# Reordering two projections, two evictions and the routing work inside the steps of a fused adaLN, attention and mixture-of-experts kernel

## The chip, the core and the metric

The kernel runs on one core of a Trainium2 chip. The metric is the device time of one execution in microseconds (us), the median of three runs. The core has five engines that run their own instruction streams in program order and meet at semaphores: TensorE (PE; its weight loads are listed as PEld), VectorE (DVE), ScalarE (ACT), GpSimd (POOL) and SyncE (SP), which here only issues DMAs.

## The reference, cut to what matters

```python
x: (8, 512, 128)                                  # 8 batches, 512 tokens
mod = silu(c) @ wmod                              # sa, ca, ga, sb, cb, gb per batch
h = layernorm(x) * (1 + ca) + sa
q, k, v = einsum('bsx,xAnh->Abnsh', h, w)         # 16 heads of 64
a = (q + q_bias) @ k.T * h**-0.5
a = a + relative_causal((q + q_bias) @ emb.T)     # sinusoid positions, 32 frequencies
o = softmax(where(mask, a, -1e9)) @ v
x = x + ga * (o @ out_kernel + out_bias)
h = layernorm(x) * (1 + cb) + sb
score = softmax(h @ Wg + bg)                      # 16 experts, top 1, capacity 256
x = x + gb * expert(h)[slot] * gate               # dropped where over capacity
```

The relative term is folded into the key product: each query row carries 64 further features (made from the "positional product" g), each key row 64 sines and cosines.

## The kernel before, in words

The attention is 64 **steps** j = 8b + a: batch b from 0 to 7, pair of heads a from 0 to 7. "Step a" below means that pair in any batch. A step has eight **tiles** k = 0 to 7: head k // 4 of the pair, query block 3, 2, 1, 0 (512, 384, 256, 128 keys wide). The stages of different steps overlap, each engine going through its own `step` function:

- TensorE (`step`, L933): for each tile the scores (`scores`, L823: three fp32r products of high and low parts, L835, and for query block 0 one plain fp32 product, L832), the transposes of step j-1's probabilities (L845), and once per step `project_v` (L820), `project_out` of step j-2 (L872), `project_q` of step j+1 (L797, ahead of tile 3), `project_k` of step j+1 (L797, behind tile 6) and `weighted`, probabilities times values of step j-1 (L865, behind tile 7). In even steps `project_g` (L797, operands named gwhi, gwlo) makes the positional product for two later steps, between tile 7 and `weighted`. Small products of the second half of the layer stand in single places: `turn_x` (step 2, tile 3), `turn_a` (1, 5), `turn_h` (3, 5), `logits` (4, 4; L893), `places` (5, 4).
- VectorE (`step`, L1367): for each tile the mask and row maximum (`scores`, srow and nmax, L1167), then `evac_q` (qx, L1191, tiles 3 and 4), `recip` of the first head (L1179, tile 4), pieces of the other work by (a, k): `residual` (1, 3), `residual2` (1, 7), `xhat1` (1, 5 and 6), `gating` (4, 5; L1257 to L1261), `low` (vlo, 4, 6), `place` (5, 5; L1280 to L1285), `route` and `index` (6, 1 and 2). Behind the tiles: `low_k(j+1, 0)` (klo, L1206), `evac_g` (g, L1200), `recip` of the second head, `evac_g`.
- ScalarE (`step`, L643): for each tile the exponential (`exps`, L612), evictions of transposes (`evac_pt`, L621), `normed` (hn, L565, step 2 behind tile 4), `second` (h2T, L631, step 3 behind tile 6); `evac_k(j+1, 0)` (khi and kx, L578 and L579) behind tile 6 and `evac_k(j+1, 1)` behind tile 7, then `evac_o`.
- GpSimd (`turn`, L458): splits queries into high and low parts (`split_q`, L445 and L447), divides the probabilities (`divide`, L454), and for the experts `modulate`, `gated` and the indirect stores of rows (`scatter`, L437), two tiles of 128 rows in step 6 and two in step 7, on its own DMA queue.
- SyncE: `spread` (L295) sends g to the query tiles for each step; stores and weight loads between.

What joins them around the change. PSUM bank `prb[0]` holds first the query product, then the key product: `project_k` waits until both `evac_q` have read it (`qe`). Bank `prb[1]`, also called `xtb`, holds in turn the value product, the small products and the positional product: `project_g` waits for `normed` (`hn`) in step 2, for the first instruction of `gating` (`lge`) in step 4, for `evac_v` (`ve`) otherwise. Score tile k needs tile k-2 to have been read by VectorE (`tt`), there being two score banks. Tile 0 of a step waits for the first half of the low queries (`ql`, at least 2j+1) and of the low keys (`kl`, at least 2j+1), which `low_k(j, 0)` of the step before sets; `low_k` needs `evac_k` (`ke`), and this needs `project_k` (`kp`).

Ahead of the steps TensorE runs loops of 128x128 bf16 products with no use but to keep it busy (`idle`, L758 to L761): 36, then 30, then 16 of them (L788), the last loop ahead of the first query product. Behind the steps a tail finishes the last batch and then runs the 16 experts.

Of the kernel before, what the change touches and what calls it, by code (L numbers as in the profile page):

```python
# [41 lines left out]
NJ = B * PAIRS  # L42
# [32 lines left out]
def program(nc, x_d, wall_d, wv_d, cols_d, wo_d, bo_d, wg_d, bg_d, w1_d, w2_d, b2_d, wmod_d,  # L75
            consts_d, ktab_d, gtab_d, out_d):
    ctx = ExitStack()
    with ctx:
# [115 lines left out]
        s = {n: sem("s_" + n) for n in names}  # L194
# [174 lines left out]
        def _(gp):  # L369
# [88 lines left out]
            def turn(b, first, last):  # L458
                for a in range(PAIRS):
                    j = 8 * b + a  # L460
                    if first and a in (1, 2):
                        first_pair(a - 1)
                        copy(0, a - 1)
                    if first and a == 3:
                        low_wk(4, PAIRS, 2)
                    if not last:
                        if a == 1:
                            root(0, b + 2)
                        if a in (5, 6):
                            copy(b + 1, a - 5)  # L470
                    if not first:
                        if a == 4:
                            modulate(b)
                        if a == 5:
                            gated(b)
                        if a == 6:
                            scatter(b, (0, 1))
                        if a == 7:
                            scatter(b, (2, 3))
                    after = not (last and a == PAIRS - 1)  # L480
                    if after:
                        split_q(j + 1, 0)
                    divide(j, a % 2, 0)
                    if not first and a == 2:
                        root(1, b)
                    if after:
                        split_q(j + 1, 1)

                    divide(j, a % 2, 1, *([("scat", 64 * b)] if a == 7 and not first else []))

# [27 lines left out]
        def _(act):  # L518
# [124 lines left out]
            def step(j, par, b, a, first, last):  # L643
                before, after = not (first and a == 0), not (last and a == PAIRS - 1)
                for k in range(8):
                    if before and 1 <= k < 6:
                        evac_pt(j - 1, k)
                    exps(j, par, k)
                    if not before:
# [11 lines left out]
                    if k == 6 and a == 3 and not first:  # L661
                        second(b)
                    if after and k == 6:
                        evac_k(j + 1, 0)
                    if k == 6 and a == 4 and not first:
                        gates(b)
                if after:
                    evac_k(j + 1, 1)
                if before:
# [59 lines left out]
        def _(pe):  # L729
# [48 lines left out]
            def turn_x(n, out=xtb):  # L778

                pe.wait_ge(s["xn"], n + 1)  # L780
                for q in range(QT):
# [5 lines left out]
                      start=True, stop=True).then_inc(s["mod_mm"], 1)  # L787
            idle(16)  # L788

# [143 lines left out]
            def step(j, par, b, a, first, last):  # L933
# [4 lines left out]
                for k in range(8):  # L938
# [28 lines left out]
                    if (a, k) == (2, 3) and not last:  # L967
                        pe.wait_ge(s["ve"], j + 4)
                        turn_x(b + 1)
                    if (a, k) in ((1, 5), (3, 5), (4, 4), (5, 4)) and not first:  # L970
                        pe.wait_ge(s["ve"], 8 * B if last and a >= 5 else j + 4)
                        if last and a >= 5:
                            pe.wait_ge(s["gq"], NJ)
                        (turn_a, None, turn_h, logits, places)[a - 1](b)
                    if k == 6 and after:
                        if first and a in (0, 3):
                            pe.wait_ge(s["kwh"], 1 if a == 0 else 2)
                            pe.wait_ge(s["kwl"], 1 if a == 0 else 2)
                        pe.wait_ge(s["qe"], 2 * j + 4)
                        project_k(j + 1, n, m)  # L980
                    if not before:
                        first_step(k)
                    if k == 7 and a % 2 == 0 and j + 2 < NJ:
                        if a == 2 and not last:
                            pe.wait_ge(s["hn"], b + 2)
                        elif a == 4 and not first:
                            pe.wait_ge(s["lge"], b)
                        else:
                            pe.wait_ge(s["ve"], j + 4)
                        project_g(j // 2 + 1)  # L990
# [87 lines left out]
        def _(dve):  # L1078
# [198 lines left out]
            def place(b):  # L1277
# [3 lines left out]
                                       base[:, None, :].to_broadcast([P, QT, E]), ALU.add))  # L1281
                dve.tensor_tensor(base[:, :], base[:, :], xtb[:, QT * E:(QT + 1) * E], ALU.add).then_inc(s["prx"], 1)
                dve.wait_ge(s["prx"], b)
                link(dve.tensor_tensor(lgt[:, 0, :], lgt[:, 0, :], oh16[:, :], ALU.mult))
                link(dve.tensor_reduce(where, te(lgt[:, 0, :]), AX.X, ALU.add))  # L1285

            def route(b):

                link(dve.tensor_scalar(late, where, float(CAP), float(NOWHERE), ALU.is_ge, ALU.mult))
# [41 lines left out]
            def after_attention(b, a, k):  # L1331
# [9 lines left out]
                if (a, k) in ((3, 1), (3, 2)):  # L1341
                    xhat2(b, range(2 * k - 2, 2 * k))
                if (a, k) == (4, 5):
                    gating(b)
# [15 lines left out]
            def step(j, par, b, a, first, last):  # L1360
                before, after = not (first and a == 0), not (last and a == PAIRS - 1)
                for k in range(8):
# [23 lines left out]
                    if not last:  # L1386
                        before_attention(b + 1, a, k)
                if after:
                    low_k(j + 1, 0)
                places = a % 2 == 0 and j + 2 < NJ  # L1390
                if places:
                    evac_g(j // 2 + 1, 0)
                recip(j, par, 1)
                if places:
                    evac_g(j // 2 + 1, 1)

            def low_wo():
# [151 lines left out]
```

## Time and profile before

| | us |
|---|---|
| median of 3 runs | 932.68 |
| lowest, highest | 932.37, 938.14 |
| profiled execution, its own time | 937.85 |
| span of the profiled execution | 935.7 |
| TensorE busy | 884.9 (95% of the span) |
| VectorE, ScalarE, GpSimd busy | 701.6, 664.4, 584.4 |
| mean granted clock of TensorE | 0.983 |

The span runs from the first to the last instruction on the core; the execution's own time is 2.15 us more. The granted clock is a share of full speed (2.4 GHz). All times in the trace count from the start of the span. A step is read from its first score product (L835 behind the last L865) to the next one. The steps take up the span from about 25 to 833 us; the tail and the experts the rest.

### The profile page before, as it was taken

Reading aid. Unit: us, or ns where it says so; the run is one execution under the profiler, and the core shown is the slowest. Engines: PE = TensorE matmul, PEld = TensorE weight load, DVE = VectorE, ACT = ScalarE, POOL = GpSimd, SP = SyncE. Lnnn points to the kernel's source line nnn. Section 1 sums busy time; section 2 is a strip of 40 time slices with the busy share of each in tenths; the row PEclk is TensorE's granted clock in tenths of the full one; section 3 lists DMA queues with packets and bytes.
Section 4 is the critical chain, followed back from the end, with each engine's and each line's share of the span. In section 5 each row is a group of like instructions: output and inputs, shape, how many; then the busy total and the mean of one; then the engine's idle time right before and its main releaser. Section 6 shows DMA issues by size and latency. Waiting matters only on the chain. (4 is left out here: it accounts for less than half of the span.)

```text
span 935.7 us, 18012 instructions
## 1 busy us (share of the span) xinstructions
PE 884.9 (95%) x5515; PEld 676.6 (72%) x5515; DVE 701.6 (75%) x2115; ACT 664.4 (71%) x1843; POOL 584.4 (62%) x917
## 2 busy tenths in 40 slices
PE   7799999999999999999999999999999999998994
PEld 6666777777777777777777767777677777666994
DVE  3678778787887778787878787877877777853784
ACT  3587777877778777877787778777787777750551
POOL 3365655777557766667577765776676757553354
PEclk7799999999999999999999999999999999999998
DMA  7223332112010111011100111010101110005671
GB/s 285 57 80 91 91 86 57 46 46 69 18 37 24 49 32 38 19 40 41 43 23 23 48 33 28 19 42 23 43 18 29 34 43 23 24 16 194 221 219 42
DMA packets 36513, 56.01 MB, mean 60 GB/s; under 512 B 7447, under 2 KB 21512, under 8 KB 36161
## 3 DMA queue, kind: packets, MB, share of 16 engines
q1 hardware_dynamic: 32624, 46.16, 17.5%
q0 software_dynamic: 3072, 5.94, 1.8%
q10 hardware_dynamic: 720, 2.75, 0.9%
q8 instruction: 45, 0.74, 0.3%
q14 instruction: 52, 0.42, 0.1%
HBM read 23.96 MB, written 16.82 MB: 44 GB/s over the span
## 5 line engine op out<-in xcount | busy, mean ns | idle before, releaser
L612 ACT ACTIVATE prob<-srow,nmax 128x512 f32<-128x512 f32 (+3 forms) x512 | 286.2, 559 | 150.6 <-DVE nmax L1167 147.7
L1167 DVE CUSTOM_DVE_ANT_0 srow<-bank,consts 128x512 f32<-128x512 f32 (+3 forms) x512 | 247.0, 488 | 111.1 <-issue 98.3
L454 POOL TENSOR_SCALAR prob<-prob,rsum 128x128 f32<-128x128 f32 (+3 forms) x512 | 263.3, 532 | 46.7 <-DVE rsum L1179 45.1
L845 PE MATMUL bank<-consts,prob 128*128 128x128 f32 x1280 | 201.8, 272 | 0.4 <-POOL prob L454 0.2
L621 ACT ACTIVATE pt<-bank 128x384 f32<-128x384 f32 x318 | 159.5, 502 | 22.2 <-PE bank L845 18.0
L845 PEld LDWEIGHTS bank<-consts,prob 128*128 128x128 f32 x1280 | 158.4, 141 | 23.0 <-POOL prob L454 1.1
L835 PE MATMUL bank<-khi,qhi 128*128 128x512 f32 (+2 forms) x384 | 158.2, 412 | 15.9 <-POOL qlo L447 13.2
L445 POOL CAST qhi<-qx 128x384 fp32r<-128x384 f32 x128 | 68.3, 534 | 167.4 <-PE bank L835 115.9
L865 PE MATMUL bank<-pt,v 128*64 128x512 f32 (+3 forms) x1024 | 152.0, 439 | 0.1
L447 POOL TENSOR_TENSOR qlo<-qx,qhi 128x384 fp32r<-128x384 f32 x128 | 128.9, 1007 | 10.8
L1206 DVE SCALAR_TENSOR_TENSOR klo<-bank,khi 64x512 fp32r<-64x512 f32 x128 | 88.0, 687 | 58.1 <-ACT kx L579 56.1
L835 PE MATMUL bank<-khi,qlo 128*128 128x512 f32 (+2 forms) x384 | 130.4, 339 | 0.0
L835 PE MATMUL bank<-klo,qhi 128*128 128x512 f32 (+2 forms) x384 | 130.1, 339 | 0.0
L865 PEld LDWEIGHTS bank<-pt,v 128*64 128x64 f32 x1024 | 68.0, 136 | 84.0 <-issue 70.3
L612 ACT ACTIVATION_READ_ACCUMULATOR prob<-srow,nmax 128x1 f32 x512 | 96.9, 189 | 0.0
L835 PEld LDWEIGHTS bank<-khi,qhi 128*128 128x128 f32 x384 | 73.0, 190 | 32.9 <-POOL qlo L447 18.6
L1191 DVE TENSOR_SCALAR qx<-bank,pbias 64x512 f32<-64x512 f32 x126 | 94.0, 746 | 2.1
L578 ACT ACTIVATE khi<-bank 64x512 fp32r<-64x512 f32 x128 | 74.8, 584 | 7.6 <-PE bank L797 6.0
L835 PEld LDWEIGHTS bank<-khi,qlo 128*128 128x128 f32 x384 | 72.7, 189 | 5.6
L835 PEld LDWEIGHTS bank<-klo,qhi 128*128 128x128 f32 x384 | 73.8, 192 | 2.8
L797 PE MATMUL bank<-hhi,whi 128*128 128x512 f32 x118 | 57.3, 486 | 6.7 <-DVE qx L1191 2.8
L832 PEld LDWEIGHTS bank<-kx,qx 128*128 128x128 f32 x256 | 44.0, 189 | 21.5 <-DVE nmax L1167 15.2
(193 smaller groups left out, 1475.5 us busy)
## 6 DMA issues: line engine op xcount, KB each, us to landing
qx<-g SPq DMA_DIRECT2D x252, 64.0 KB, 2.0
xbuf<-fill SPq DMA_DIRECT2D x16, 385.0 KB, 4.3
x<-xbuf SPq DMA_DIRECT2D x16, 385.0 KB, 3.6
raw<-in_w SPq DMA_DIRECT2D x16, 256.0 KB, 3.0
prob<-in_w SPq DMA_DIRECT2D x16, 256.0 KB, 4.3
out<-row SPq DMA_DIRECT2D x8, 256.0 KB, 2.6
x<-in_x SPq DMA_DIRECT2D x1, 1792.0 KB, 14.9
modb<-mod_rows SPq DMA_DIRECT2D x8, 192.0 KB, 3.7
```

What stands on the lines that cost most here:

```text
L445: gp.tensor_copy(qhi[:, h, :], qraw(j, h)[:, P:S]).then_inc(s["qh"], 1)
L447: gp.tensor_tensor(qlo[:, h, :], qraw(j, h)[:, P:S], qhi[:, h, :], ALU.subtract).then_inc(s["ql"], 1)
L454: end = gp.tensor_scalar(part, part, rsum[:, par, 4 * h + q:4 * h + q + 1], 1.0, ALU.mult, ALU.mult)
L578: act.activation(khi[0:HD, h, :], prb[0][h * HD:(h + 1) * HD, :], ACT.Copy, scale=C_QKV)
L612: act.activation(prob[:, par, h, QOFF[q]:QOFF[q] + P * (q + 1)], srow[:, k % 4, 0:P * (q + 1)], ACT.Exp, bias=nmax[:, par, k:k + 1], scale ...
L621: act.activation(pt[:, h, KOFF[g]:KOFF[g] + GW[g]], source[:, 0:GW[g]], ACT.Copy)\
L835: last = pe.matmul(out, a[:, h, (q - 1) * P:q * P], b[:, h, 0:P * (q + 1)], start=(i == 0), stop=(i == 2))
L845: last = pe.transpose(out[:, n * P:(n + 1) * P], prob[:, par, h, QOFF[q] + k * P:QOFF[q] + (k + 1) * P], ident)
L865: last = pe.matmul(otb[h * HD:(h + 1) * HD, k * P:S], v[:, g, k, at + h * HD:at + (h + 1) * HD], pt[:, h, KOFF[k]:KOFF[k] + S - k * P], st ...
L1167: dve.tensor_tensor_reduce(out=srow[:, k % 4, 0:w], in0=scb[k % 2][:, 0:w], in1=mask[:, S - w:S], scale=-1.0, scalar=BIG, op0=ALU.add, op1 ...
L1191: dve.tensor_scalar(qraw(j, h)[0:HD, :], prb[0][own, :], pbias[own, a:a + 1], CQ, ALU.add, ALU.mult)\
L1206: dve.scalar_tensor_tensor(klo[0:HD, h, :], prb[0][h * HD:(h + 1) * HD, :], C_QKV, khi[0:HD, h, :], ALU.mult, ALU.subtract).then_inc(s["kl ...
```

## The change

TensorE: in even steps `project_g` moves from behind tile 7 to behind tile 6, and `project_k` from behind tile 6 to behind tile 7, directly ahead of `weighted`; odd steps stay. `logits` moves from tile 4 to tile 3 of step 4. In the very first step `project_g` waits for the first value eviction in place of the fourth. The last warm-up loop has 40 products in place of 16.

ScalarE: in odd steps `evac_k(j+1, 0)` goes ahead of the exponential of tile 6; in even steps both `evac_k` stand behind tile 7.

VectorE: `gating` moves from tile 5 to tile 4 of step 4; the wait and the last two instructions of `place` (step 5) move to the front of `route` (step 6); in even steps `low_k(j+1, 0)` goes behind both `evac_g` and `recip`.

GpSimd: the four indirect stores of a batch, two each in steps 6 and 7, become one each in steps 6 and 7 and in steps 0 and 1 of the next batch, save for the last group taken inside the steps; the wait for them moves with them.

```diff
@@ GpSimd, turn
-                        if a == 6:
-                            scatter(b, (0, 1))
-                        if a == 7:
-                            scatter(b, (2, 3))
+                        if a >= 6:
+                            scatter(b, (2 * a - 12, 2 * a - 11) if last else (a - 6,))
+                    if b > 1 and a < 2:
+                        scatter(b - 1, (a + 2,))
...
-                    divide(j, a % 2, 1, *([("scat", 64 * b)] if a == 7 and not first else []))
+                    divide(j, a % 2, 1, *([("scat", 64 * b - 64)] if a == 1 and b > 1 else []))
@@ ScalarE, step
+                    if after and k == 6 and a % 2:
+                        evac_k(j + 1, 0)
                     exps(j, par, k)
...
-                    if after and k == 6:
-                        evac_k(j + 1, 0)
                     if k == 6 and a == 4 and not first:
                         gates(b)
                 if after:
-                    evac_k(j + 1, 1)
+                    for h in range(a % 2, 2):
+                        evac_k(j + 1, h)
@@ TensorE, before the steps
-            idle(16)
+            idle(40)
@@ TensorE, step
-                    if (a, k) in ((1, 5), (3, 5), (4, 4), (5, 4)) and not first:
+                    if (a, k) in ((1, 5), (3, 5), (4, 3), (5, 4)) and not first:
...
-                    if k == 6 and after:
+                    if k == 7 - a % 2 and after:
...
-                    if k == 7 and a % 2 == 0 and j + 2 < NJ:
+                    if k == 6 and a % 2 == 0 and j + 2 < NJ:
                         if a == 2 and not last:
                             pe.wait_ge(s["hn"], b + 2)
                         elif a == 4 and not first:
                             pe.wait_ge(s["lge"], b)
                         else:
-                            pe.wait_ge(s["ve"], j + 4)
+                            pe.wait_ge(s["ve"], j + 4 if before else 1)
                         project_g(j // 2 + 1)
@@ VectorE, place and route
+
+            def route(b):
+
                 dve.wait_ge(s["prx"], b)
                 link(dve.tensor_tensor(lgt[:, 0, :], lgt[:, 0, :], oh16[:, :], ALU.mult))
                 link(dve.tensor_reduce(where, te(lgt[:, 0, :]), AX.X, ALU.add))
-
-            def route(b):
-
@@ VectorE, after_attention
-                if (a, k) == (4, 5):
+                if (a, k) == (4, 4):
                     gating(b)
@@ VectorE, step
-                if after:
+                places = a % 2 == 0 and j + 2 < NJ
+                if after and a % 2:
                     low_k(j + 1, 0)
-                places = a % 2 == 0 and j + 2 < NJ
                 if places:
                     evac_g(j // 2 + 1, 0)
                 recip(j, par, 1)
                 if places:
                     evac_g(j // 2 + 1, 1)
+                if after and a % 2 == 0:
+                    low_k(j + 1, 0)
```

## Rows read from the trace of the kernel before

**Rows 1.** windows over the eight steps (pairs of heads 0 to 7) of batch 3; columns: stretch, length, busy us per engine, clock

```profile
332.67:345.39 12.72, 12.55 (x76) 9.10 (x74) 9.92 (x34) 9.76 (x29) 7.42 (x13) 1.00 0.05 12
345.39:358.48 13.09, 12.14 (x77) 9.12 (x75) 11.42 (x31) 9.45 (x27) 8.37 (x14) 1.00 0.15 36
358.48:371.47 12.99, 12.83 (x78) 9.50 (x78) 9.78 (x34) 10.20 (x29) 7.32 (x13) 1.00 0.19 42
371.47:383.81 12.34, 11.83 (x77) 9.06 (x75) 9.63 (x29) 9.93 (x27) 8.13 (x14) 1.00 0.15 37
383.81:396.63 12.82, 12.82 (x82) 9.96 (x82) 10.12 (x28) 10.38 (x31) 9.98 (x14) 1.00 0.03 7
396.63:409.06 12.43, 11.84 (x81) 8.97 (x79) 10.59 (x36) 9.44 (x27) 8.65 (x14) 1.00 0.16 39
409.06:421.49 12.43, 12.29 (x74) 9.04 (x74) 9.53 (x31) 9.94 (x29) 8.28 (x14) 1.00 0.11 37
421.49:433.25 11.76, 11.62 (x73) 8.66 (x71) 8.56 (x25) 9.23 (x27) 10.13 (x16) 1.00 0.23 67
```

**Rows 2.** timeline of the end of step 3; columns: start, us, engine, line, what

```profile
380.92 2.37 PE L865 MATMUL bank<-pt,v 128*64 128x512 f32 x16
...
381.10 0.49 ACT L612 ACTIVATE prob<-srow,nmax 128x256 f32<-128x256 f32 x1
...
382.25 0.57 ACT L578 ACTIVATE khi<-bank 64x512 fp32r<-64x512 f32 x1
...
383.02 0.68 DVE L1206 SCALAR_TENSOR_TENSOR klo<-bank,khi 64x512 fp32r<-64x512 f32 x1 [1.60 <-ACT kx L579]
...
383.77 0.19 PEld L835 LDWEIGHTS bank<-khi,qhi 128*128 128x128 f32 x1 [0.72 <-POOL qlo L447]
```

**Rows 3.** timeline of VectorE in step 5

```profile
405.99 0.25 DVE L1284 TENSOR_TENSOR lgt<-lgt,oh 128x64 f32<-128x64 f32 x1
...
406.52 0.42 DVE L1167 CUSTOM_DVE_ANT_0 srow<-bank,consts 128x256 f32<-128x256 f32 x1
...
408.26 0.68 DVE L1206 SCALAR_TENSOR_TENSOR klo<-bank,khi 64x512 fp32r<-64x512 f32 x1 [1.10 <-ACT kx L579]
```

**Rows 4.** timeline of the second half of step 2

```profile
367.14 0.76 ACT L565 ACTIVATE hn<-bank,modT 128x512 f32<-128x512 f32 x1
...
367.23 0.19 PEld L797 LDWEIGHTS bank<-hhi,whi 128*128 128x128 f32 x1 [0.37 <-DVE qx L1191]
...
368.28 0.48 PE L797 MATMUL bank<-hhi,gwhi 128*128 128x512 f32 x1
```

**Rows 5.** timeline of the second half of step 4

```profile
390.47 0.69 DVE L1167 CUSTOM_DVE_ANT_0 srow<-bank,consts 128x512 f32<-128x512 f32 x1 [0.17 <-issue]
390.50 0.96 PE L893 MATMUL bank<-wg,h2T 128*128 128x16 f32 x8
...
392.22 0.56 DVE L1167 CUSTOM_DVE_ANT_0 srow<-bank,consts 128x384 f32<-128x384 f32 x1
...
392.71 0.22 DVE L1257 TENSOR_TENSOR lgt<-bank,bg 128x64 f32<-128x64 f32 x1
...
393.30 0.38 PE L832 MATMUL bank<-kx,qx 128*128 128x128 f32 x2
...
393.72 0.41 DVE L1167 CUSTOM_DVE_ANT_0 srow<-bank,consts 128x256 f32<-128x256 f32 x1
...
394.32 2.38 PE L865 MATMUL bank<-pt,v 128*64 128x512 f32 x16
...
396.06 0.73 DVE L1200 SCALAR_TENSOR_TENSOR g<-bank,gbias,gtab 128x512 f32<-128x512 f32 x1
```

**Rows 6.** windows at the start of the program, with the granted clock (PEclk)

```profile
12.57:15.98 3.41, 1.36 (x17) 0.90 (x16) 1.01 (x1) 3.35 (x7) 2.42 (x2) 1.00 0.89 336
15.98:33.05 17.07, 14.65 (x74) 12.08 (x75) 8.42 (x16) 4.99 (x16) 4.30 (x6) 0.50 0.25 103
```

**Rows 7.** timeline of TensorE, the last warm-up loop

```profile
12.86 1.07 PE L761 MATMUL bank<-ones 128*128 128x128 bf16 x16
```

## The prediction

> **What bounds the kernel now.** I read first the share of the span by engine: TensorE is busy 95%, no other engine over 75%. Then I cut one batch into its eight steps [rows 1]. They repeat from batch to batch within 0.05 us, so one batch stands for seven. The reader is to see that TensorE is full in steps 2, 4 and 6, and short by 0.95, 0.51 and 0.59 us in steps 1, 3 and 5; step 7 has no such hole and takes 11.76 us. So gains can only come from the holes, and every wait that is put into steps 2 and 4 is paid in full.
>
> What makes the holes? In step 3 the timeline shows TensorE coming to the next step's first scores at 383.77, with a wait that the view puts down to the low queries [rows 2]. By the code the first tile needs only their first half, which was made 4 us before. The instruction that ends 0.07 us ahead is klo, the low keys: 383.02 + 0.68 = 383.70. They wait for khi and kx, which ScalarE takes up at 382.25, behind two other activations, though the key product was long done. `weighted` started at 380.92 and takes 2.30 (394.32 to the next step at 396.62, [rows 5]), so TensorE was free at 383.22. The hole is 0.58. In step 5 it is 12.43 - 11.76 = 0.67 [rows 1], again behind klo [rows 3]. In step 1 VectorE is busy 11.42 of 13.09 us [rows 1], and without a pause in the second half, so ScalarE's order can't help there.
>
> **The change part by part.**
>
> *Odd steps, high keys first.* In step 3 khi can start where the exponential now starts, at 381.10 in place of 382.25 [rows 2]: klo ends 1.15 us sooner, more than the hole of 0.58, and TensorE's 2.30 of `weighted` set the end. Same in step 5, hole 0.67. The two delayed exponentials end about 0.6 us into the next step; the first row maximum is due about 1.1 us into a step and ScalarE has some 1 us of idle time ahead of its first exponential, which covers them. Gain 7 x 0.58 + 7 x 0.67 = 8.8 us. Batch 0's odd steps give about 0.5 (0 at the least, two holes like these at the most). Step 7 has no hole: nothing. Step 1: nothing, VectorE's other work covers it.
>
> *Step 2, the positional product behind tile 6.* It writes the bank that `normed` reads, and hn ends at 367.14 + 0.76 = 367.90 [rows 4]. Nothing of the change makes hn earlier. The key product now starts at 367.23; in its place TensorE holds until 367.94, and what follows it (tile 7, the other product, `weighted`) is the same work in another order. Of the 0.71, 0.05 to 0.1 was spent waiting at tile 7 anyway. Cost 0.62, in batches 0 to 6 (the last has no `normed`): +4.3.
>
> *Step 4, logits and gating one tile earlier.* `logits` takes TensorE from 390.50 to 391.32 [rows 5], and now stands ahead of tile 4: its row maximum on VectorE moves from 390.47 to 391.29. From there VectorE goes through evac_q and `recip` to tile 5, 392.22 - 390.47 = 1.75 later, so to 393.04; but `gating` now stands ahead of tile 5, and takes 392.71 to 393.72, 1.01. Tile 5's maximum starts at 394.05 and is done at 394.61. Tile 7 reuses that score bank and waits for it: 394.66 in place of 393.30 [rows 5]. From tile 7 to the step's end stand a product and `weighted`, 1.02 to 1.08 and 2.30: the step ends at 398.04, not 396.62. Cost 1.42. The second chain is as long: VectorE in the new order has tile 6, vlo, tile 7, g, `recip`, g, klo behind 394.05, some 3.9 us by their pitches in the same step, and ends at 398.0. Seven batches: +9.9. Batch 0 has no gating, but in its step 4 VectorE's other pieces already end the step with klo, and klo goes behind two g and a `recip` (0.66 + 0.1 + 0.65, estimated from the row of g): +1.4. The bound from below for both steps is 0, should the held time be covered by something that I don't see; from above 0.4 more per step 4, if both chains add. I take the middle since both chains give the same number.
>
> *Other even steps.* In steps 0 and 6 tile 7 waits for tile 5's maximum before and after; a product stands between and one behind, whichever it is. Nothing in step 0. Low keys last: g is now read before the key product is even done, so klo follows about 12.4 us into a step of 12.72 [rows 1], hidden behind `weighted` with about 0.2 to spare (that cover gone, each 0.1 costs 0.1 in 14 steps). In step 6 the two instructions taken from `place` cost 406.52 - 405.99 = 0.53 [rows 3] in a stretch with about 0.35 of idle time: +0.18 in six batches, 1.1. In the last batch's step 6 there is no positional product to trade with, and the key product moves from beside a wait to the path: 0.9. In step 5 that same 0.53 is in front of klo no more, but the floor of 11.76 is TensorE's.
>
> *GpSimd.* It is busy 7.42 and 8.37 us in steps 0 and 1 [rows 1] and idle in the middle of each, waiting for queries; one indirect store of about 1 us fits. The wait for the stores moves to step 1's second `divide`, by when they have landed. What is behind it, the transposes of step 2, has 2 us to spare. The stores also stand behind nothing on SyncE's queue. g is ready earlier, but SyncE's copies of it wait for the same scores: nothing.
>
> *Warm-up.* Sixteen products took 1.07 us [rows 7] at the full 2.4 GHz; 24 more take some 1.3, inside the pause before the first query product. From 12.57 to 15.98 the clock was full while TensorE worked only 1.36 of 3.41 us, and then it was at its half level, 1.2 GHz, for 17.07 us, 14.65 of them busy [rows 6]. At full clock those would take half: 7.3 us is the most to be had, -0.35 (the loop at half clock reaching past the pause) the least. I take 5.2, which is also how far the profiled execution, 937.85, lies above the median of 932.68; I read that difference as this stretch, and so credit the median itself with nothing more. The Trainium skill, page "TensorE: Matmul & The Clock Gate", section "What's actually happening", says that warming up costs time and not a number of products, that its point moves from run to run, and advises not to fit to a count; by it the loop brings nothing dependable, and an execution like the profiled one would end at 946.2.
>
> Sum: -8.8 - 0.5 + 4.3 + 9.9 + 1.4 + 1.1 + 0.9 = +8.3. Against the profiled execution: 937.85 + 8.3 - 5.2 = 941.0; against the median: 932.68 + 8.3 + 0 = 941.0.
>
> **The rivals.** (1) *The waits in steps 2 and 4 are covered, and it gets faster.* It decides on whether hn and `gating` come before TensorE has finished tile 6 (366.8 in step 2). For it: VectorE and ScalarE are idle 25% of each step. Against it: both chains start from TensorE's own tile 4 and have nothing idle inside. Then 4.3 and 9.9 fall away: 941.0 - 14.2 = 926.8, and 925.4 without batch 0's. (2) *Low keys end every even step late.* If the estimate of their slack is short by 0.3 to 0.4: 14 to 20 steps, +5: 946. For it: the order puts them behind four instructions; against: the sum leaves 0.2. (3) *The half clock stays in the median*: 941.0 + 5.2 = 946.2. (4) *The start gives more than 5.2*: up to 3 more, 938. (5) *Odd steps don't gain*, since the delayed exponentials hold up ScalarE: +8.8, 950; against it the idle time ahead of each first exponential.
>
> **How the numbers follow.** A change of 1% is what a measurement of this kernel can tell from none: 923.4 and 942.0. The forecast has 0.60 (936 to 946; 0.37 of it below 942.0, 0.23 above), rival 1 has 0.13 (0.04 below 923.4), rival 2 0.08, rival 3 0.07, rival 4 0.08, rival 5 0.04. Faster 0.04; same 0.37 + 0.09 + 0.08 = 0.54; slower 0.23 + 0.08 + 0.07 + 0.04 = 0.42. The range is 932 to 947: it leaves out most of rival 1, and rival 5.
>
> **What would show it.** In the new trace steps 3 and 5 take 11.8 us, with no wait at their end; step 2 takes 13.6, TensorE idle ahead of the positional product until hn; step 4 takes 14.2 to 14.4, with two holes, one ahead of the positional product (behind `gating`'s first instruction) and one ahead of tile 7; steps 0, 1, 6 and 7 take 12.7, 13.1, 12.6 and 11.8. The granted clock at the start is full for longer. Wrong would be a step 4 under 13.3, or a step 3 over 12.2: then VectorE's order or ScalarE's doesn't set what I say it does.

## The result, and the profile after

The changed kernel takes 940.77 us in the median of 8 runs (938.08 to 942.94); the kernel before, beside it, 933.67. The ratio is 1.0067 [1.0046, 1.0089]: slower by 7.1 us, and within 1%. The prediction was 941.0.

The profiled execution of the changed kernel took 942.51 us, with a span of 940.6 and a mean clock of 0.986; before it was 937.85, 935.7 and 0.983. The page's line of shares shows how little an average tells here:

```profile
PE 885.7 (94%) x5539; PEld 675.8 (72%) x5539; DVE 700.1 (74%) x2115; ACT 664.0 (71%) x1843; POOL 587.4 (62%) x917
```

All engines but GpSimd are within 1.5 us of their sums of before, and so the time is in the waits. The windows over the eight steps of batch 2 (same columns as [rows 1]) show where:

```profile
231.61:244.31 12.70, 12.43 (x75) 9.03 (x73) 10.47 (x34) 9.79 (x29) 8.84 (x15) 1.00 0.10 28
244.31:257.42 13.11, 12.12 (x76) 9.12 (x75) 10.95 (x30) 9.70 (x27) 9.19 (x15) 1.00 0.19 52
257.42:271.02 13.60, 12.71 (x77) 9.59 (x77) 10.38 (x34) 10.18 (x29) 7.84 (x14) 1.00 0.14 38
271.03:282.79 11.76, 11.76 (x76) 9.04 (x75) 8.91 (x27) 9.37 (x26) 7.27 (x13) 1.00 0.15 36
282.79:296.81 14.02, 13.37 (x83) 9.95 (x81) 10.69 (x31) 10.96 (x33) 10.92 (x17) 1.00 0.05 12
296.82:308.59 11.77, 11.77 (x80) 8.94 (x79) 9.31 (x31) 9.31 (x26) 7.79 (x13) 1.00 0.14 33
308.59:321.23 12.64, 12.39 (x75) 9.03 (x73) 10.50 (x33) 9.72 (x29) 8.53 (x15) 1.00 0.09 27
321.23:332.99 11.76, 11.63 (x72) 8.65 (x70) 8.15 (x24) 9.23 (x26) 8.33 (x14) 1.00 0.19 52
```

Steps 3 and 5 have lost their holes (TensorE 11.76 of 11.76, before 12.34 and 12.43). Step 2 grew from 12.99 to 13.60, step 4 from 12.82 to 14.02. Over all batches, from the first score of one step to that of the next:

| step | 0 | 1 | 2 | 3 | 4 | 5 | 6 | 7 | sum |
|---|---|---|---|---|---|---|---|---|---|
| predicted | 0 | 0 | +4.3 | -4.3 | +11.3 | -4.9 | +2.0 | 0 | +8.3 |
| measured | -0.11 | +0.09 | +4.69 | -5.29 | +9.52 | -4.94 | +2.19 | -0.36 | +5.8 |

(The sums run from batch 0's step 2 on and are in us; each number is rounded; batch 0's -0.5 is halved over steps 3 and 5.) The stretch ahead of batch 0's step 2 took 54.29 us for 56.02, and what follows the steps 0.8 more.

Three cells of the measured row hold something that is not the change. In single steps VectorE takes up one row maximum 0.36 us later than in the same step of the other batches, and the step is longer by as much: step 4 of batch 4 and step 7 of batch 6 in the kernel before (13.19 and 12.12 us), step 2 of batch 3 in the changed one (13.96). Every kernel here with the stores and `place` as before has these two, every one with them as changed has that one; no row says what the cause is. Without it step 2 is at +4.3, step 4 at +9.9, step 7 at 0 and the sum at +6.2.

**End of step 3**, the timeline of batch 3 after:

```profile
382.25 2.38 PE L866 MATMUL bank<-pt,v 128*64 128x512 f32 x16
...
382.43 0.57 ACT L578 ACTIVATE khi<-bank 64x512 fp32r<-64x512 f32 x1
...
383.06 0.50 ACT L612 ACTIVATE prob<-srow,nmax 128x256 f32<-128x256 f32 x1
...
383.20 0.68 DVE L1207 SCALAR_TENSOR_TENSOR klo<-bank,khi 64x512 fp32r<-64x512 f32 x1 [0.44 <-ACT kx L579]
...
384.56 0.50 PE L836 MATMUL bank<-khi,qhi 128*128 128x512 f32 x1
```

klo used to end 0.07 us ahead of the next scores [rows 2]. Now it ends at 383.88, 0.68 ahead, and the scores come 2.31 behind the start of `weighted`: TensorE's own work sets the end.

**Second half of step 2**, batch 2:

```profile
266.10 0.76 ACT L565 ACTIVATE hn<-bank,modT 128x512 f32<-128x512 f32 x1
...
266.91 0.19 PEld L798 LDWEIGHTS bank<-hhi,gwhi 128*128 128x128 f32 x1 [1.10 <-ACT hn L565]
...
267.82 0.19 PEld L798 LDWEIGHTS bank<-hhi,whi 128*128 128x128 f32 x1
```

The step's first score starts at 257.42. hn ends at 266.86, 9.44 us into it, where it ended before (367.90 - 358.48 = 9.42, [rows 4, 1]), but the product with gwhi is now the one that is next in line, and it waits until 266.91.

**Second half of step 4**, batch 3 again; its first score starts at 384.56:

```profile
390.25 0.96 PE L894 MATMUL bank<-wg,h2T 128*128 128x16 f32 x8
...
392.14 0.69 DVE L1168 CUSTOM_DVE_ANT_0 srow<-bank,consts 128x512 f32<-128x512 f32 x1 [1.07 <-issue]
...
393.87 0.23 DVE L1258 TENSOR_TENSOR lgt<-bank,bg 128x64 f32<-128x64 f32 x1
394.01 2.60 POOL L454 TENSOR_SCALAR prob<-prob,rsum 128x128 f32<-128x128 f32 x4 [1.22 <-DVE rsum L1180]
394.13 0.22 DVE L1261 TENSOR_REDUCE rsm<-lgt 128x4 f32<-128x64 f32 x1
...
394.15 0.50 PE L798 MATMUL bank<-hhi,gwhi 128*128 128x512 f32 x1 [0.61 <-DVE lgt L1258]
394.38 0.23 DVE L1262 TENSOR_TENSOR lgt<-lgt,rsm 128x64 f32<-128x64 f32 x1
...
394.54 0.56 DVE L1168 CUSTOM_DVE_ANT_0 srow<-bank,consts 128x384 f32<-128x384 f32 x1
...
395.15 0.30 PEld L833 LDWEIGHTS bank<-kx,qx 128*128 128x128 f32 x2 [0.47 <-DVE nmax L1168]
...
395.36 0.69 DVE L1121 TENSOR_TENSOR vlo<-hn,vhi 128x512 fp32r<-128x512 f32 x1
...
396.28 2.38 PE L866 MATMUL bank<-pt,v 128*64 128x512 f32 x16
...
397.69 0.67 DVE L1207 SCALAR_TENSOR_TENSOR klo<-bank,khi 64x512 fp32r<-64x512 f32 x1
...
398.58 0.50 PE L836 MATMUL bank<-khi,qhi 128*128 128x512 f32 x1
```

The chain is the one that was forecast: tile 4's maximum behind `logits` (7.58 us into the step; 390.47 - 383.81 = 6.66 before, [rows 5, 1]), then `gating` in front of tile 5, whose maximum ends at 395.10, and tile 7's scores behind it. There are the two holes: 0.61 ahead of the positional product, and one ahead of tile 7, where the weight load waits 0.47 and the product some 0.2 (the third product of the row of three starts at 394.72 and takes 0.23 until the next could follow, at 394.95; tile 7 comes at 395.16). klo ends at 398.36, 0.22 ahead of the next scores.

### The profile page after: what moved, and what is told of

It reads as the page before. It is cut to its first block and busy times, and to the rows that moved or that the text cites. A ratio compares the mean times of both kernels' runs of the same rounds, so it can differ in the third digit from the quotient of the medians.

```text
span 940.6 us, 18077 instructions
## 1 busy us (share of the span) xinstructions
PE 885.7 (94%) x5539; PEld 675.8 (72%) x5539; DVE 700.1 (74%) x2115; ACT 664.0 (71%) x1843; POOL 587.4 (62%) x917
## 5 line engine op out<-in xcount | busy, mean ns | idle before, releaser
L454 POOL TENSOR_SCALAR prob<-prob,rsum 128x128 f32<-128x128 f32 (+3 forms) x512 | 267.7, 541 | 39.4 <-DVE rsum L1180 33.9
L445 POOL CAST qhi<-qx 128x384 fp32r<-128x384 f32 x128 | 65.7, 513 | 169.0 <-PE bank L836 99.8
L836 PE MATMUL bank<-khi,qhi 128*128 128x512 f32 (+2 forms) x384 | 158.3, 412 | 11.3 <-POOL qlo L447 7.1
L833 PE MATMUL bank<-kx,qx 128*128 128x128 f32 x256 | 54.8, 296 | 5.5 <-DVE nmax L1168 5.1
```

The lines of the kernel that those rows point to most:

```text
L454: end = gp.tensor_scalar(part, part, rsum[:, par, 4 * h + q:4 * h + q + 1], 1.0, ALU.mult, ALU.mult)
L833: last = pe.matmul(out, qraw(j, h)[:, 0:P], kx[:, h, :], start=True, stop=True)
L836: last = pe.matmul(out, a[:, h, (q - 1) * P:q * P], b[:, h, 0:P * (q + 1)], start=(i == 0), stop=(i == 2))
```

## The experiments

Each is an edit of the kernel before or of the changed one; its ratio is against the kernel before, in runs on the same chip. The kernel before itself took 933.67 to 935.28 us from group to group of runs, so two experiments are best compared by their ratios.

### Odd steps alone (the kernel before, with the high keys ahead of the seventh exponential)

```diff
+                    if after and k == 6 and a % 2:
+                        evac_k(j + 1, 0)
                     exps(j, par, k)
...
-                    if after and k == 6:
+                    if after and k == 6 and a % 2 == 0:
                         evac_k(j + 1, 0)
```

> The kernel before with one part of the change: in odd steps ScalarE evicts the high keys ahead of the exponential of tile 6; nothing else. My theory: the holes at the end of steps 3 and 5 are the wait for the low keys and go entirely: steps 3 and 5 take 11.76 us (12.34 and 12.43 before), step 1 stays at 13.1, the even steps at 12.72, 12.98, 12.82, 12.43. With batch 0 that is about -10, a ratio of 0.989 (923.5 us against 933.7). Rival: the gain needed the new order of the even steps as well (the delayed exponentials would otherwise meet the positional product's evictions): steps 3 and 5 above 12.0 and less than -4.

925.7 us, 0.9917 [0.9889, 0.9944]. The windows over steps 3 and 5 of one batch:

```profile
263.27:275.03 11.76, 11.76 (x77) 9.04 (x75) 9.55 (x29) 9.37 (x26) 7.77 (x14) 1.00 0.14 36
287.89:299.65 11.76, 11.76 (x80) 8.95 (x79) 10.59 (x36) 9.40 (x27) 8.22 (x14) 1.00 0.15 36
```

All steps together take 8.76 us less: 4.35 in step 3, 4.84 in step 5, and 0.4 given back elsewhere. So this part of the change is a gain by itself, and the rest of it costs 14 to 15 us.

### Logits and gating both back (the changed kernel, tiles 4 and 5 again)

```diff
-                    if (a, k) in ((1, 5), (3, 5), (4, 3), (5, 4)) and not first:
+                    if (a, k) in ((1, 5), (3, 5), (4, 4), (5, 4)) and not first:
...
-                if (a, k) == (4, 4):
+                if (a, k) == (4, 5):
                     gating(b)
```

> The changed kernel with the logits back at tile 4 and gating back at tile 5 of step 4; all else as changed, so the positional product still waits for gating's first instruction. My theory: gating ahead of tile 5's row maximum is what makes step 4 long. Without it the positional product starts at about 9.2 us in the step, and the step takes 13.3 us (14.02 in the changed kernel, 12.82 before): -5, a ratio to before of 1.002. Rival: the order of the two products makes step 4 long, whichever tile gating stands at: 13.9 to 14.1, ratio unchanged at 1.007.

935.68 us, 1.0018 [1.0003, 1.0034]. Step 4 takes 13.49:

```profile
280.56:294.05 13.49, 13.19 (x84) 10.09 (x82) 11.13 (x31) 11.21 (x34) 11.26 (x18) 1.00 0.05 12
```

About half of step 4's loss is gone. Of the other 0.67 over the 12.82 of [rows 1], some 0.5 is the positional product, which stands one place earlier and waits for `gating` to read its bank: its weight load stands idle 0.41 us, until 289.76. The last 0.17 is klo, last on VectorE. It ends at 293.94, 0.10 ahead of the next step's first score at 294.04, and from the first product of `weighted`, 291.57, to that score it is 2.47, where TensorE's own work takes 2.30.

### Even order back (the changed kernel, keys and products in even steps as before)

```diff
-                    if k == 7 - a % 2 and after:
+                    if k == 6 and after:
...
-                    if k == 6 and a % 2 == 0 and j + 2 < NJ:
+                    if k == 7 and a % 2 == 0 and j + 2 < NJ:
...
-                if after and a % 2:
+                if after:
                     low_k(j + 1, 0)
```

(and ScalarE's high keys to match, and the very first step's `project_g` waiting for the fourth value eviction again).

> The changed kernel with the even steps' order as before on all engines (key product behind tile 6, positional product behind tile 7, high and low keys first); gating and logits one tile early, the split place, the stores and the warm-up loop as changed. My theory: step 2 falls from 13.60 to 12.98, step 4 stays at 14.0 since tile 7 still waits for tile 5's row maximum behind gating, the last batch's step 6 falls by 0.9: -5.5, a ratio to before of 1.001. Rival: the order is what costs in step 4 too: 12.8, ratio 0.992.

934.11 us, 1.0000 [0.9984, 1.0017]. The windows over steps 2 and 4:

```profile
253.27:266.26 12.99, 12.82 (x78) 9.51 (x78) 9.78 (x34) 10.07 (x29) 7.31 (x13) 1.00 0.14 39
278.02:292.06 14.04, 13.39 (x84) 9.97 (x82) 10.16 (x31) 10.96 (x33) 10.49 (x15) 1.00 0.05 12
```

Step 2's loss is gone whole, step 4's not at all: with `logits` ahead of tile 4 and `gating` ahead of tile 5, tile 7's wait for tile 5's maximum sets step 4, wherever the products stand. So step 4 has two causes, one enough for 13.49 and the other for 14.02, and they don't add.

### Step 2's order alone back (the changed kernel)

```diff
-                    if k == 7 - a % 2 and after:
+                    if k == (6 if a == 2 else 7 - a % 2) and after:
...
-                    if k == 6 and a % 2 == 0 and j + 2 < NJ:
+                    if k == (7 if a == 2 else 6) and a % 2 == 0 and j + 2 < NJ:
```

> The changed kernel, with TensorE's two products of step 2 alone put back (key product behind tile 6, positional product behind tile 7); the evictions behind the tiles stay as changed. My theory: the positional product no longer stands at the normed activation, and step 2 falls from 13.60 to 13.0; all else as changed: -4.4, a ratio to before of 1.002 to 1.003. Rival: the cost of step 2 is klo standing behind g and recip on VectorE, not the wait for hn: then step 2 stays at 13.4 or more.

936.18 us, 1.0023 [1.0011, 1.0034]; the window over step 2:

```profile
254.10:267.08 12.98, 12.82 (x78) 9.49 (x78) 10.41 (x34) 10.09 (x29) 7.32 (x13) 1.00 0.15 39
```

With only TensorE's order in that step restored, the 0.62 is gone; klo stays last on VectorE and costs nothing. (Batch 0's step 2 keeps 0.41 of its 0.62; why is open.)

### Logits alone back (the changed kernel, gating still at tile 4)

```diff
-                    if (a, k) in ((1, 5), (3, 5), (4, 3), (5, 4)) and not first:
+                    if (a, k) in ((1, 5), (3, 5), (4, 4), (5, 4)) and not first:
```

> The changed kernel with the logits alone back at tile 4 of step 4; gating stays at tile 4 on VectorE, ahead of tile 5. This parts step 4's cost into the 0.8 us by which the logits delay tile 4's row maximum and the gating ahead of tile 5's. My theory: both lie on one chain to tile 7, and TensorE had 0.5 us to spare at that point; without the logits' 0.8 tile 7 starts at 9.7, step 4 takes 13.1 (14.02 with both, 12.82 before): -6.4, ratio to before of 1.000. Rival: gating alone makes the step long (over 13.6).

934.53 us, 0.9996 [0.9981, 1.001]:

```profile
280.60:293.73 13.13, 13.11 (x84) 9.90 (x82) 10.68 (x31) 11.06 (x33) 10.89 (x17) 1.00 0.05 12
```

0.9 us of step 4's 1.20 was `logits` in front of tile 4, which is as long as the wait that it put into VectorE's chain (390.47 to 391.29 in the prediction). `gating` at tile 4 leaves only the other 0.3, and in this order of the products it does better there than at tile 5: with both back step 4 took 13.49, since the positional product then had to wait for `gating`, and here its weight load comes at 289.31 with no wait shown. So the part of the change that made step 4 long was above all the move of `logits`.

### A longer warm-up loop alone (the kernel before)

```diff
-            idle(16)
+            idle(40)
```

> The kernel before with 40 products in place of 16 in the last warm-up loop, nothing else. My theory: only the stretch ahead of step 2 moves, earlier by 2 (0 to 5) us, because the granted clock is at its full level for part of the first products; ratio 0.998. Rival 1: the loop changes nothing that lasts (1.000). Rival 2: the whole stretch at half clock goes: -5 and more, ratio 0.994 or less.

933.52 us, 0.9991 [0.9972, 1.001]: not to be told from nothing. The profiled execution reached step 2 at 50.45 us with the clock full, but the odd-keys kernel, with 16 products, reached it at 50.08 with the clock full too. Four of the twelve executions have a mean clock of 0.995 or more, and one of the 29 of the kernel before beside them; that is a hint that the longer loop helps at times, too weak to show in the median.

### Stores spread, and `place` cut in two (the kernel before)

```diff
-                dve.wait_ge(s["prx"], b)
-                link(dve.tensor_tensor(lgt[:, 0, :], lgt[:, 0, :], oh16[:, :], ALU.mult))
-                link(dve.tensor_reduce(where, te(lgt[:, 0, :]), AX.X, ALU.add))
...
+                dve.wait_ge(s["prx"], b)
+                link(dve.tensor_tensor(lgt[:, 0, :], lgt[:, 0, :], oh16[:, :], ALU.mult))
+                link(dve.tensor_reduce(where, te(lgt[:, 0, :]), AX.X, ALU.add))
                 link(dve.tensor_scalar(late, where, float(CAP), float(NOWHERE), ALU.is_ge, ALU.mult))
```

(with the three edits of the stores on GpSimd as in the change).

> The kernel before with the indirect stores of the expert rows spread over steps 6, 7, 0 and 1, and place's last two instructions moved to route; nothing else. My theory: the stores are free on GpSimd either way; route, longer by 0.53, holds tile 3's row maximum in step 6, which takes 12.65 (12.43 before): +1.4, ratio 1.0015. Rival: the stores in steps 6 and 7 held something up, and spreading them gains: step 7 under 11.7, or ratio under 0.999.

932.2 us, 0.9977 [0.9963, 0.999]: a miss, it is faster. The windows over steps 5 and 6, and the end of step 5 in the same kernel's timeline:

```profile
290.92:302.74 11.82, 11.82 (x80) 8.95 (x79) 10.10 (x34) 9.42 (x27) 8.30 (x14) 1.00 0.14 35
302.74:315.37 12.63, 12.50 (x75) 9.08 (x74) 9.94 (x33) 9.80 (x29) 8.45 (x15) 1.00 0.09 27
```

```profile
299.95 0.30 PEld L832 LDWEIGHTS bank<-kx,qx 128*128 128x128 f32 x2 [0.28 <-DVE nmax L1167]
...
300.22 0.42 DVE L1167 CUSTOM_DVE_ANT_0 srow<-bank,consts 128x256 f32<-128x256 f32 x1
...
301.96 0.68 DVE L1206 SCALAR_TENSOR_TENSOR klo<-bank,khi 64x512 fp32r<-64x512 f32 x1 [1.09 <-ACT kx L579]
...
302.71 0.19 PEld L835 LDWEIGHTS bank<-khi,qhi 128*128 128x128 f32 x1 [0.21 <-issue]
```

Without the two instructions tile 6's maximum starts 0.27 us behind the start of tile 7's scores; before it was 0.86 (406.52 against 405.66), with `place` ending between them [rows 3]. The seventh exponential, khi and klo follow it, and step 5's hole is all but gone: 11.82 for 12.43. Step 6 takes 0.2 more, as was forecast. (The stores and `place` were not run apart; that the gain is `place`'s is read from this timeline, and steps 7, 0 and 1, where the stores moved, stayed within 0.05 us.) The two parts of the change, high keys first and `place` cut, each buy the same hole. Together they buy it once, and the cost in step 6 is left over.

### The changed kernel with its first step in the order of before

```diff
-                    if k == 7 - a % 2 and after:
+                    if k == (7 - a % 2 if before else 6) and after:
...
-                    if k == 6 and a % 2 == 0 and j + 2 < NJ:
+                    if k == (6 if before else 7) and a % 2 == 0 and j + 2 < NJ:
```

(and the keys on ScalarE and VectorE and the wait for the value evictions to match; `before` is false in the first step only).

> The changed kernel with the very first step alone in the order of before on all three engines (key product behind tile 6, positional product behind tile 7, keys evicted first). In the changed kernel's trace TensorE pauses 2.1 us in front of step 1 and the granted clock then falls to half from 39.9 to 43.3 us; before, the pause was 1.4 us and the clock stayed. My theory: the order of the first step costs 1 to 2 us of the start: ratio 1.005 against 1.007 for the changed kernel. Rival: the start is as scattered without it and nothing changes.

938.78 us, 1.0048 [1.003, 1.0065]. The steps took what they take in the changed kernel; the start took 49.87 us, not 54.29. The windows of the changed kernel from 16 to 48 us, its timeline of TensorE there, and the windows of this one:

```profile
16.00:32.00 16.00, 13.14 (x76) 10.74 (x75) 9.51 (x19) 5.02 (x18) 4.22 (x5) 0.68 0.25 106
32.00:48.00 16.00, 12.89 (x63) 10.33 (x64) 10.70 (x36) 10.47 (x27) 9.16 (x16) 0.89 0.44 133
```

```profile
37.05 0.40 PE L821 MATMUL bank<-wvhi,vlo 128*128 128x512 f32 x1
39.58 0.47 PE L836 MATMUL bank<-khi,qhi 128*128 128x512 f32 x1 [2.13 <-POOL qlo L447]
```

```profile
16.00:32.00 16.00, 12.06 (x91) 9.70 (x92) 11.48 (x27) 7.71 (x25) 4.16 (x5) 1.00 0.33 129
32.00:48.00 16.00, 12.28 (x67) 9.13 (x67) 12.64 (x38) 11.56 (x32) 13.12 (x22) 1.00 0.39 120
```

In the second of these windows the four kernels with the changed first step have a granted clock of 0.79 to 0.89, the nine others (the kernel before and eight experiments) one of 0.97 to 1.00. But the two ratios' intervals overlap, and each kernel's start is one execution. That the first step's order costs some 2 us in the median is likely from this, not shown. (In the changed kernel's trace the half level stands from 40.1 to 43.5 us; the times in the expectation are 0.2 early.)

### Going on from the odd steps: step 1's VectorE work moved

To the odd keys, this adds:

```diff
-                    if (a, k) == (2, 3) and not last:
+                    if (a, k) == (2, 4) and not last:
...
-                if (a, k) in ((1, 5), (1, 6)):
+                if n == 1 and (a, k) in ((1, 5), (1, 6)):
                     xhat1(n, range(2 * k - 10, 2 * k - 8))
+                if n > 1 and (a, k) == (1, 2):
+                    xhat1(n, range(0, 2))
...
+                if a == 1 and 0 < b and not last:
+                    xhat1(b + 1, range(2, 4))
```

> The kernel before with the odd steps' part of the change, and two moves of my own: in step 1 the four normalising instructions of xhat1 leave tiles 5 and 6 (two go to tile 2, two behind the step's last reciprocal), and in step 2 turn_x goes from tile 3 to tile 4. My theory: step 1 is bound by VectorE between tile 3 and klo, so it falls from 13.10 to 12.25; step 2's scores of tile 4 come 0.36 sooner, so it falls from 12.98 to 12.7. With the odd steps' 9.2: -16, ratio 0.983. Rival: the work only moves on, and the normalising instructions hold step 2's first row maximum: step 2 above 12.98, ratio 0.988 or more.

920.29 us, 0.9851 [0.983, 0.9872]; the windows over steps 1 and 2:

```profile
239.92:252.14 12.22, 12.08 (x76) 9.10 (x74) 10.62 (x30) 9.23 (x26) 7.98 (x14) 1.00 0.13 32
252.14:264.86 12.72, 12.72 (x80) 9.52 (x78) 10.60 (x36) 10.32 (x30) 7.68 (x14) 1.00 0.17 48
```

Step 1's hole of 0.95 is nearly closed (13.09 before) once its last maxima don't stand behind half of the normalisation, and step 2 gains 0.27 as well. All steps together take 16.0 less, as forecast. The kernel before had this floor in its own trace: in the last batch, which has no next batch to normalise for, its steps 1 and 2 take 12.21 and 12.71.

### Positional product first where nothing else waits for it: steps 0 and 6

This one adds to the last kernel, in steps 0 and 6 alone, the exchanged products, with tile 5's maximum put ahead of the second `evac_q` and of `recip`:

```diff
-                    if k in (3, 4) and after:
-                        evac_q(j + 1, (a + 1) % PAIRS, k - 3)
+                    swap = a in (0, 6) and before and j + 2 < NJ
+                    if k == 3 and after:
+                        evac_q(j + 1, (a + 1) % PAIRS, 0)
+                    if k == (5 if swap else 4) and after:
+                        evac_q(j + 1, (a + 1) % PAIRS, 1)
...
-                    if k == 4:
+                    if k == (5 if swap else 4):
                         recip(j, par, 0)
```

> The same as the step 1 and 2 kernel, and in steps 0 and 6 alone (without the first step) the changed kernel's order: positional product behind tile 6, key product behind tile 7, evictions of the keys last. With it tile 5's row maximum goes ahead of evac_q's second half and the first reciprocal on VectorE. My theory: the order in itself gives nothing since tile 7 waits for tile 5's maximum; with that maximum 0.95 sooner TensorE runs through, steps 0 and 6 fall from 12.72 and 12.43 to 12.2 and 11.95: -7 more, ratio 0.976. Rival: the late key product then waits for evac_q, or the low keys come too late: steps 0 and 6 stay within 0.1 of 12.7 and 12.4.

915.12 us, 0.9798 [0.9781, 0.9815]. Step 0 takes 12.46 and step 6 12.18, each 0.25 more than expected. The end of step 6 in its timeline of VectorE:

```profile
306.71 0.75 DVE L1205 SCALAR_TENSOR_TENSOR g<-bank,gbias,gtab 128x512 f32<-128x512 f32 x1
...
307.76 0.75 DVE L1205 SCALAR_TENSOR_TENSOR g<-bank,gbias,gtab 128x512 f32<-128x512 f32 x1
...
308.43 0.67 DVE L1211 SCALAR_TENSOR_TENSOR klo<-bank,khi 64x512 fp32r<-64x512 f32 x1
```

klo, behind both g, ends at 309.10, 0.10 ahead of the next step's first score, which is how near it comes wherever it is what TensorE waits for. How much that wait costs shows only from the start of `weighted`: to the next score it is 2.34 us here and 2.60 in step 0, for the 2.30 of TensorE's own work, so klo holds up step 6 by 0.04 and step 0 by 0.30. The last experiment puts klo between the two g, and the high keys between the exponentials:

```diff
                     evac_g(j // 2 + 1, 0)
+                if after and swap:
+                    low_k(j + 1, 0)
                 recip(j, par, 1)
```

> The swap kernel, in whose steps 0 and 6 the keys' low part is last on VectorE, with two moves back in those two steps: ScalarE evicts the first keys between the exponentials of tiles 6 and 7, and klo stands between the two evictions of g, ahead of the second reciprocal. My theory: there klo, ready 0.1 us ahead of the next step's first scores, is the last thing that sets steps 0 and 6 (12.46 and 12.18); with klo 0.5 sooner they take 12.2 and 11.95: -3.4 on top, ratio 0.976 against 0.980. Rival: TensorE has no slack left there, and the steps stay.

912.32 us (910.86 to 914.27), 0.9758 [0.974, 0.9776]: the fastest, 2.4% under the kernel before and, by the two ratios, 3.1% under the changed one.

The same klo in its step 6, and the windows over its steps 0 and 6:

```profile
308.28 0.68 DVE L1209 SCALAR_TENSOR_TENSOR klo<-bank,khi 64x512 fp32r<-64x512 f32 x1 [0.44 <-ACT kx L579]
```

```profile
223.91:236.07 12.16, 12.16 (x75) 9.12 (x73) 9.94 (x34) 9.64 (x29) 6.71 (x13) 1.00 0.05 13
297.40:309.55 12.15, 12.15 (x76) 9.18 (x74) 9.88 (x31) 9.97 (x29) 8.36 (x14) 1.00 0.14 45
```

Step 0 gave the 0.30. Step 6 gave 0.03 and missed the 11.95 that was expected: there TensorE is full, and what is left is its own work.

## Why the prediction was right, point by point

**The odd steps** were right: holes behind klo, closed by taking khi first (the odd keys alone, 0.9917; 4.35 and 4.84 in steps 3 and 5, for 4.3 and 4.9 with batch 0's share). Rival 5 fell with it: the delayed exponentials held nothing up. Batch 0's step 3 gave 1.23 in the changed kernel and 0.28 with the odd keys alone; why the other even order helps there isn't settled.

**Step 2** was right in place and size: hn at 9.44 us into the step, the next product 0.05 behind it, 13.60 for the 13.6 forecast. Restoring TensorE's order in this step alone gave 12.98.

**Step 4** had the right chain and the wrong size. The term that failed is the 1.01 us taken for `gating` in the new place, and with it 1.42 per step; measured 1.20 in batches 1 to 7, and 14.02 where I had 14.2 to 14.4. `gating` took 394.54 - 393.87 = 0.67, 0.34 less, while tile 4's maximum came 0.92 later for the 0.82 forecast, which took 0.10 back. The second chain, VectorE's, was not as long as the first: klo ended 0.22 ahead of the next score. The row that I took the 1.01 from has an operation in it that was slow where it stood, as the timeline of the kernel before shows:

```profile
392.34 2.05 POOL L454 TENSOR_SCALAR prob<-prob,rsum 128x128 f32<-128x128 f32 x4 [0.33 <-DVE rsum L1179]
...
392.96 0.22 DVE L1260 TENSOR_REDUCE rsm<-lgt 128x4 f32<-128x64 f32 x1
393.21 0.58 DVE L1261 TENSOR_TENSOR lgt<-lgt,rsm 128x64 f32<-128x64 f32 x1
```

The same product takes 0.58 there and 0.23 after, though nothing of it has changed, only when it meets GpSimd's divides; those took 2.05 before and 2.60 after. The sizes came in smaller for VectorE and larger for GpSimd. That this is one cause was read from four kernels (the changed one and the one with logits alone back: 0.23 and 2.60; before and with both back: 0.58 and 2.05), not tested by itself. Batch 0's step 4 cost 1.44 for the 1.4 forecast.

**Steps 0 and 6** were right: step 0 unchanged, klo's end 0.35 ahead of the next score there and 0.22 in step 4, where 0.10 is the least, so rival 2 fell in the changed kernel (it came true, by 0.17, in step 4 with logits and gating both back); step 6 +0.22 for +0.18, the last batch's +0.91 for +0.9. What I didn't see is that taking the two instructions out of step 5 is worth 0.59 by itself. I said that they are in front of klo no more and that TensorE's floor holds, which is true only beside the other edit.

**Rival 1** (both waits covered) fell: TensorE stands idle at both places. The terms of the steps come to +5.8 for +8.3, or +6.2 without the single late maxima: step 4 has 1.4 of the difference and step 3 1.0. Those maxima also make one sentence of mine too strong: the steps repeat within 0.05 us in most batches, but not in two steps of the kernel before (0.36 longer each), nor in the last batch, whose steps 0, 1 and 2 are shorter (12.48, 12.21 and 12.71).

**The start** was the weak part. Against the profiled execution I forecast -5.2 and the trace shows -1.7, and the median, to which I credited nothing, is where the sum held (+7.1 for +8.3). That before's profiled execution lay above the median for its half clock at the start holds: kernels with a full clock there reach step 2 at 49.9 to 50.5 us, that one at 56.02. The repeated runs say the same: of 29 executions of the kernel before beside the first experiments, the five fastest up to 932.29 us have a mean clock of 0.992 to 0.995, the eight slowest from 935.26 on one of 0.984 to 0.986. That the longer loop removes it is not supported (0.9991 [0.9972, 1.001]): the clock was full in kernels with 16 products, and at half for part of the start in the changed one with 40. The Trainium skill, page "TensorE: Matmul & The Clock Gate", section "What's actually happening", advises not to fit to a count of products, as the point moves from run to run and the whole is under 1% of a span; the runs agree, with 6 us of 933 as the most. So that 941.0 came out nearly exact was luck in part, since two terms were off: the steps were 2.5 too dear, and 1.3 of it came back outside them (the start's order, the end, or chance). Rival 3, the half clock in the median, fell (940.77 for 946.2), and rival 4 too, a start that gives more than 5.2.

**Left open**: the 0.8 us behind the last step (other kernels show -0.4 to +2.2 there), the first step's share in the clock, and what makes a single row maximum 0.36 us late.

## What to carry to other kernels

Cut the span into the steps that repeat, and ask of each hole which instruction ends last there: moving one operation past another paid 0.6 to 0.7 us per step where it was that one, and cost 0.6 to 1.2 where TensorE had been full. When a move puts a product in front of a bank that another engine reads, or a read in front of the maximum that frees a bank, follow that chain to the end of the step; and where two edits aim at one hole, count it once. Test the parts of such a bundle apart: here one of them alone was worth 0.8%, inside a change that lost 0.7%.

## What the runs showed of the hardware

- A VectorE product of 128x64 with both inputs in SBUF took 0.58 us beside GpSimd's divides and 0.23 in another phase with them; vlo (128x512) 0.87 and 0.69; GpSimd's four divides of 128x128 2.05 and 2.60. The Trainium skill, page "SBUF — State Buffer", section "Who interferes with whom", says that these two engines share one pair of ports, locked whole by one of them at a time. The trace agrees: in step 4 the two VectorE operations together took 0.53 us less than before, GpSimd's four divides 0.55 more.
- After a pause of TensorE of 2.13 us that ended at 39.58 us, the clock fell to its half level from 40.1 to 43.5 us in the changed kernel; before, a pause of 1.36 us that ended at 40.84 left it full.
- One program's time differs from execution to execution with its clock: 29 executions of the kernel before took 930.57 us (mean clock 0.993) to 937.62 (0.984), which is as much as the whole change was worth. The profiled executions, one for each kernel, reached batch 0's step 2 between 49.9 and 56.0 us.
- In single steps VectorE takes up one row maximum 0.36 us late (in the changed kernel at 366.40, in batch 3 only). Such steps count in a sum over batches as if they were the change's.
